# A ternary network inside a two-layer decoder: the second block's convolutions follow the first block's at five slots' distance

## The reference

```python
def act_quant(x):
    scale = 127.0 / jnp.clip(jnp.max(jnp.abs(x), axis=-1, keepdims=True), 1e-05)
    return jnp.clip(jnp.round(x * scale), -128, 127) / scale
def bit_linear(x, w):                      # both operands are quantized
    return jnp.einsum('bsd,hd->bsh', act_quant(x), weight_quant(w))
h = bit_linear(x, w1)                      # 256 -> 1024 channels
h = depthwise_conv1d(h.transpose(0, 2, 1), conv_w, conv_b)   # 3 taps along the rows
h = jax.nn.silu(h.transpose(0, 2, 1))
return bit_linear(h, w2)                   # 1024 -> 256 channels
```

## Time and profile before

| quantity | value |
| --- | --- |
| median of 3 runs | 1972.89 us (1972.87 to 1973.23) |
| profiled execution | 1966.51 us |
| its span (first to last instruction) | 1964.7 us |
| busy in the span: TensorE, VectorE, ScalarE, GpSimd | 87%, 71%, 52%, 23% |
| mean granted clock of TensorE | 0.937 |

### The profile page before, as it was taken

The page is one execution under the profiler, slowest core; times in us unless marked ns, Lnnn a source line. Parts: engine busy times, 40 slices in busy tenths (PEclk is TensorE's granted clock), DMA queues, the critical chain, the costliest instruction groups (busy, mean ns, idle before and its releaser), DMA issues.

```text
span 1964.7 us, 34748 instructions
## 1 busy us (share of the span) xinstructions
PE 1718.0 (87%) x12889; PEld 1250.4 (64%) x12889; DVE 1388.7 (71%) x4883; ACT 1014.9 (52%) x2641; POOL 460.9 (23%) x501
## 2 busy tenths in 40 slices
PE   3688888889898878999999999999989999979708
PEld 1446666667653455666766766676778989864307
DVE  7877888888436886787777567777447676753785
ACT  5555655555547534545555345555345454533752
POOL 4000000000000223334434234434322323220003
PEclk7798888998998979999999999999999999999859
DMA  5100000000000102000000000000333434200001
GB/s 165 43 1 1 2 1 2 1 1 1 2 1 14 30 22 71 1 1 1 1 1 1 1 1 1 1 2 1 100 87 76 93 70 98 66 1 0 0 0 43
DMA packets 86078, 49.56 MB, mean 25 GB/s; under 512 B 40223, under 2 KB 83669, under 8 KB 85717
## 3 DMA queue, kind: packets, MB, share of 16 engines
q1 hardware_dynamic: 80195, 47.18, 9.2%
q10 hardware_dynamic: 5714, 0.16, 0.2%
HBM read 45.24 MB, written 2.10 MB: 24 GB/s over the span
## 4 chain that ended last, share of the span: by engine, by line
PE 53%; DVE 30%; ACT 12%; issue 3%; POOL 2%; POOLq 0%; ACTq 0%; DVEq 0%
PE PS L2135 6%; DVE nx L775 5%; DVE sq L784 5%; ACT px L1875 5%; PE PS L1805 4%; PE PS L1817 3%; PE PS L1830 3%; PE PS L1845 3%; PE PS L2571 3%; PE PS L2199 3%; PE PS L1791 3%; DVE px L1957 2%; DVE cm L1938 2%; PE PS L2155 2%; ACT pT L1888 2%
## 5 line engine op out<-in xcount | busy, mean ns | idle before, releaser
L1875 ACT ACTIVATE px<-PS,cnm 128x896 f32<-128x896 f32 (+7 forms) x256 | 189.4, 757 | 294.4 <-DVE cnm L1940 294.4
L1982 POOL TENSOR_SCALAR px<-px,crl 128x640 f32<-128x640 f32 (+7 forms) x128 | 238.1, 1870 | 371.5 <-DVE crl L1951 371.5
L784 DVE TENSOR_SCALAR sq<-nx 128x4 f32<-128x4 f32 x1024 | 174.8, 171 | 31.4
L775 DVE TENSOR_TENSOR_SCAN nx<-sq 128x6 f32<-128x6 f32 x1024 | 173.6, 170 | 32.0 <-POOL sq L914 0.9
L1938 DVE TENSOR_REDUCE cm<-PS 128x1 f32<-128x512 f32 (+3 forms) x224 | 153.4, 685 | 27.3 <-PE PS L1805 27.0
L1817 PE MATMUL PS<-ident,px 128*128 128x128 f32 x1152 | 156.2, 280 | 15.2 <-ACT pT L1888 12.2
L2239 ACT ACTIVATE YT<-YT,xnm 128x154 f32<-128x154 f32 x256 | 104.8, 413 | 93.4 <-DVE xnm L2270 93.4
L1817 PEld LDWEIGHTS PS<-ident,px 128*128 128x128 f32 x1152 | 123.7, 141 | 43.0 <-ACT pT L1888 30.4
L1805 PE MATMUL PS<-kT,qT 64*128 64x512 f32 (+3 forms) x768 | 147.9, 503 | 0.4
L1830 PEld LDWEIGHTS PS<-pT,V 128*64 128x64 f32 x2304 | 125.2, 137 | 34.4 <-issue 32.5
L198 POOL TENSOR_SCALAR rstd<-mv 128x1 f32<-128x1 f32 x80 | 31.2, 390 | 484.1 <-DVE mv L176 484.0
(11 more groups left out here) (340 smaller groups left out, 3844.3 us busy)
## 6 DMA issues: line engine op xcount, KB each, us to landing
xbs<-in_fside_Bx16xSxS SPq DMA_DIRECT2D x8, 1232.0 KB, 6.7
fsrc<-in_fside_Bx16xSxS SPq DMA_DIRECT2D x8, 1232.0 KB, 6.7
xmk<-in_mask_Bx16xSxS_bk SPq DMA_DIRECT2D x8, 308.0 KB, 8.4
fsrc<-in_mask_Bx16xSxS_bk SPq DMA_DIRECT2D x8, 308.0 KB, 8.3
X<-in_x SPq DMA_DIRECT2D x4, 512.0 KB, 6.7
w<-in_L_attn_W_ffn SPq DMA_DIRECT2D x2, 1024.0 KB, 11.8
t<-in_L_ffn_w SPq DMA_DIRECT2D x2, 1024.0 KB, 10.5
out<-xs SPq DMA_DIRECT2D x16, 128.0 KB, 1.7
```

The source lines that it names most:

```text
L775: e.tensor_tensor_scan(k.nx[:, t % 2, :], d0, d1, 0.0, ALU.mult, ALU.add).then_inc(sem("rec.scan"), 1)
L784: e.tensor_scalar(place(c % 2 * 2 * W6 + 6 * n + 7), state, 10.0, -10.0, ALU.min, ALU.max).then_inc(sem("rec.clip"), 1)
L1875: e.activation(k.px[n % 2][:, h, c0:c1], row[:, c0:c1], ACT.Exp, scale=-1.0, bias=k.cnm[:, h, slot:slot + 1], accum_out=k.cl[:, h, slot:sl ...
L1982: e.tensor_scalar(x, x, k.crl[:, 0, slot:slot + 1], None, ALU.mult).then_inc(sem("c.normal0"), 1)
```

## The change

Two entries of the order change. All four blocks now have one rule for the slot of a convolution: block 1 stands five slots behind block 0, as block 3 stands behind block 2. The maximum of block 1 goes from slot 19 to 23, and `t2.across` of block 1 from 22 to 24. What `ternary_order` derives from that entry goes with it: the second scales of block 1 and its tiles' `scale`, `round`, second product, sum and norm come two slots later.

```diff
 def conv_slot(u, j):
-    return EC * (u // 2 * 2 + 1) + j + 1 + (5 if u == 3 else u % 2 if by_tensor(j) else 0)
+    return EC * (u // 2 * 2 + 1) + j + 1 + (0, 5, 0, 5)[u]
...
     for u in range(blocks):
-        n, across = ((18, 19), (19, 22), (34, 35), (39, 40))[u]
+        n, across = ((18, 19), (23, 24), (34, 35), (39, 40))[u]
         put(n, ("t2.max", u))
         put(across, ("t2.across", u))
```

## The result

| | before | after |
| --- | --- | --- |
| median of 20 runs each (the three of before among them) | 1967.32 us | 1975.4 us |
| lowest | 1964.14 us | 1969.17 us |
| profiled execution, its span | 1966.51, 1964.7 us | 1979.34, 1977.5 us |
| mean granted clock of TensorE | 0.937 | 0.934 |

The ratio is 1.0034, with a 95% interval of 1.0024 to 1.0044: 6.7 us slower, and beyond the 0.2% that can be told apart. One run of before took 2251.56 us and is left out of the ratio. I had forecast 1974.7 us, and the median after, 1975.4, lies close to it. That is an accident of the base: the three runs before the prediction had given 1972.89, and 20 runs give 1967.32. In the difference I forecast +1.8 us, and the range of 1970.2 to 1978.6 us means -2.7 to +5.7 on that base; +6.7 came out, outside it.

The account below looks back on a forecast made before the run. No engine was full from 603 to 650 us; VectorE bound 650 to 691. Head -2.1 us, then middle and tail, put the third maximum 1.8 later: 1966.51 + 1.8 = 1968.3, plus 6.4 for typical runs, 1974.7; range 1970.2 to 1978.6.

Parts of the forecast that it names:

- Head: Ternary network up to the second maximum's end: VectorE's waits fall from 12.3 to 9.9 us, 2.1 us gained.
- Middle: Second maximum's end to tile 7's scaling: 31.9 us of VectorE work plus 1.25 for exposed norms, ending at 682.7.
- The rule of the Trainium skill: Norms of tiles 2 and 7: if GpSimd's root stood still under convolutions, 1.2 us more; not adopted.
- Tail: Tile 7's scaling to third maximum: ScalarE waits, chunk 7's convolution at low clock costs 1.7 us; maximum 1.8 us later.
- my bounds: Head: -5 to +1 us around its value; tail's clock loss: none to 3.6 us, around 1.7.
- Behind the third maximum: TensorE's next convolution: keeping full clock could bring the spreading 2.2 us earlier; counted as nothing, with 2.3 as bound.
- Beyond the stretch: From the third maximum on, all engines keep the same order, except TensorE's last transpositions of block 1.
- Mine for slower: Rival: low clock through the tail's whole chain, third maximum 3.5 us later, 1976.9 to 1979.5 us; chance 0.18.
- The clock holds: Rival in the tail: TensorE's small product in the gap suffices, or the convolution meets release early; 1972 to 1973.5; chance 0.20.
- the head gains more: Rival in slots 9 to 14: ScalarE gets ahead one SiLU earlier, 3 to 5 us more, 1968 to 1971.5; chance 0.15.

Follow-up runs that it names:

- experiment 4: Kernel before with only block 1's maximum and transposition moved, to slots 23 and 24, convolutions in their old slots; ratio to before 1.0024.
- Experiment 3: Changed kernel plus nine unread matmuls filling TensorE's gaps before the convolution of chunk 7; 1971.07 us, ratio to before 1.0022.
- Experiment 11: Kernel before with block 1's maximum in slot 21, plus unread matmuls: three in the causal gap, four before the third maximum's transposition; ratio to before 0.9978.
- experiment 7: Kernel before with one number altered: block 1's maximum in slot 21 instead of 19; ratio to before 0.9995.
- experiment 6: Changed kernel with block 1's maximum and transposition one slot earlier, in slots 22 and 23; ratio to before 1.0018.
- experiment 9: Changed kernel plus three unread matmuls in TensorE's gap in the first round of the causal part; ratio to before 1.0016.

## Why the prediction was off in the difference, step by step

In the absolute time the prediction came out right, and by luck: a base that was 5.6 us too high (1972.89 instead of 1967.32) made up for a difference that was too small, 1.8 us where the two medians lie 8.1 apart.

- *Head, right.* First maximum at 626.9 on the clock of before (626.85 predicted), first tile scaled at 641.7 (641.6), second maximum ends at 649.9 (649.5). On the way, TensorE's waiting product starts at 608.0 (607.9) and the spreading ends at 641.1 (641.0). What I had not separated is that most of the first tile's lead, 4.7 of 6.1 us, comes from the second maximum's place and not from the spread convolutions (experiment 4).
- *Middle, 0.35 too short.* Tile 7's scaling ends at 683.4, I had 682.7; 0.35 of this is the second maximum's. The exposed norms were 0.46 and 1.00 us, where I had 0.25 and 1.0. The rule of the Trainium skill that I had weighed (GPSIMD Engine Reference, section Specifications, on the shared way into SBUF and VectorE instructions with two SBUF inputs) would have made the norms of tiles 2 and 7 wait 1.0 each, if the root stood still under a convolution. The trace does not agree with that strict reading: the waits of these two are 0.46, at 670.25 and at 701.20. The power of a root does take longer there, 1.05 us as in the earlier trace rows, against 0.57 with VectorE idle (at 742.83 us in the kernel before); whether it is slowed all along or stopped for a part of one convolution, these times don't tell, so my "slowed and not stopped" was more than the row shows. By my own terms that rule would have added 1.45 us, not 1.2.
- *Tail, the step that was mis-sized.* Mechanism and order were as forecast: ScalarE waits for tile 7, the copy behind it, the convolution behind that at the low clock. I had put the loss of clock at 1.7 us, what a product lost in one row. From the convolution's start to the last sum it took 6.97 us (691.18 to 698.15), where 4.1 is the full clock (2.7, 0.45 and 0.95 in my sum): 2.9 lost. Experiment 3 confirms the size, 3.0. The 5.06 us in the earlier trace rows for the very same instruction, 2.2 more than its 2.84, was the nearer row, and the chain behind it was to be counted at the low clock as well. The convolution began 0.9 late and the way from the sum to the maximum took 0.2 more; with the 0.14 of my own sum at the full clock these are 4.1 us, not 1.8. (Nor do the ends of my range follow from my bounds: with 5 and 1 us for the head and 1.7 and 1.9 for the clock they would be 1968.0 and 1977.6.)
- *Behind the third maximum, counted at nothing, 0.7 came back.* The convolution ran at 2.74 us instead of 5.06 as I had described, but of 2.3 us only 0.7 reach the next part (4.1 us late at the maximum, 3.4 there), since the spreading then waits 1.61 us for `dg`. Experiment 11 has the same wait.
- *Beyond the stretch, the step that failed.* I had written that a delay at the network's end moves all that follows. It did not move it rigidly: 1.7 us more were lost to a low-clock stretch at the start of the causal attention, which the kernel before escaped, with 0.3 ahead of it for a wait of 0.35 us on `px` of L1875 whose reason I did not find. That each of the eight traces of a changed order, early or late, has the low stretch there is shown; why the two traces of the kernel before escape it is not. The wait on `px` is the nearest difference.
- *The rest.* 3.4 + 2.0 = 5.4 of the 6.7 us are named. They agree with the 4.6 and 5.5 us by which the groups of runs differ. The last 1.3 us may be chance, in either of two places: the low-clock stretches behind 1380, where the two traces of each kernel end 2.2 and 2.3 us apart, and the share of runs with a late opening.
- *The rivals.* Mine for slower (3.5 later at the third maximum, 1976.9 to 1979.5) had the tail nearly right, as the low clock did cover convolution, transposition and second product. But its last link did not come: the convolution of chunk 3 ran at the full clock again (2.85 us). And it had nothing of the 2.0 us beyond the network, without which the whole would not have been 6.7. "The clock holds" and "the head gains more" fall: idle times of 2.99 and 5.07 us were not bridged by one small product.

## What to carry to other kernels

When a step is moved later, look at what stands behind its last dependent on each in-order engine: here one SiLU waiting for a buffer held back a copy that it has nothing to do with, for 8.62 us. Price a gap that the change opens on TensorE by the row in which the same instruction ran at the low clock, and count every instruction of the chain behind it at that price. And compare two traces by distance from a common event over the whole program, since a change in one part can cost clock in the next, here 1.7 us; a few matmuls that nobody reads, in a gap that can't be closed, are a cheap test of this and here were part of the fastest kernel. Look at single runs too, and not only at their median: here they fall in two groups, and a median between them belongs to no run.

## What was not expected of the hardware

- The same four matmuls after the same 2.55 us of idle time took 1.98 us in the kernel before and 3.02 in experiment 7, and 3.02 in experiment 6 too, which came to that part at the time of before. The length of the idle time right ahead did not decide the clock alone.
- The low clock can end inside one convolution: it took 4.24 us in experiment 9 and 5.49 in the kernel after, with the same idle time of 5.07 to 5.08 us ahead of it, and takes 2.84 at the full clock.
- The opening of the program varied by 8.8 us between executions (593.65 to 602.4 at the first product of block 1), more than the change moved, and the whole execution with it. That is why profiled executions of two kernels can't be set against each other by their spans.
